# Two conditioned attention layers: where the mask of the second layer's scores is added

## The chip, the cores and the metric

The kernel runs on one core of a Trainium2 chip. The metric is the device time of one execution in microseconds. The core has five engines that work side by side and signal each other with semaphores: TensorE (matrix products; its results go to eight PSUM banks of 128 x 512 floats), VectorE, ScalarE, GpSimd, and SyncE, which issues the DMAs here. SBUF is the on-chip memory of 128 partitions.

## The reference

The input x is 64 sequences of 128 positions with 512 features. Two layers run one after the other, each x + h(x). The first is a linear attention of 8 heads. The second, which this case is about, is an ordinary softmax attention of 16 heads of 32 features:

```python
xn = layer_norm(x, norm_w, norm_b)
q = (xn @ q_w + q_b).reshape(Bx, Tx, H, -1)
k = (xn @ k_w + k_b).reshape(Bx, Tx, H, -1)
att = jnp.einsum('bnhl,bmhl->bnmh', q, k)
att = att + (1.0 - mask) * -1000000.0          # one value for each key position m
att = jax.nn.softmax(att, axis=2)              # over m
v = ((xn @ v_w + v_b) * src_mask[:, :, None]).reshape(Bx, Tx, H, -1)
y = jnp.einsum('bnmh,bmhl->bnhl', att, v).reshape(Bx, Tx, Dx)
h = layer_norm(y, sb_norm_w, sb_norm_b) * (1.0 + scale) + shift   # scale, shift from emb
h = jax.nn.silu(h) @ out_w + out_b
return x + h
```

## The kernel before

`setup` loads the small inputs, `layer0` runs the first layer and writes its result to a DRAM tensor, `second_weights` prepares the second layer's weights, and `layer1` runs the second layer. All work goes by pairs of sequences, 32 of them. Each engine has its own program, a hand-written order of steps (`body(i, ...)`), once for every pair; the steps of one pair's end (pair i - 1) are woven into the body of pair i. An engine runs its own instructions strictly in the order written.

All large products are of floats split into a high and a low part, three products instead of one (`project_features` L462 to L464, `project_rows` L453 to L455).

The scores of a sequence come twice in `layer1`. The first time (`scores`, L1475) they are laid out with the query position in the partitions: four banks (`S_BANKS`), the four row strips `a` of the array at the same time, each bank holding four heads side by side (128 columns each). Ahead of the products of the heads (`heads`, L1422), each bank is opened by a product of two rows of ones with two rows that hold the mask's high and low part (L1485, tile `mask_rows`), so that the mask is in the sum. VectorE then takes the negated maximum of every head (`maxima`, L1168, instruction at L1171) into `top`. TensorE transposes `top` (`shift_row`, L1490, product at L1493), ScalarE copies it to `top_T`, and the second time (`weight_scores`) the scores are computed transposed, opened by a product that adds the negated maxima (L1443); ScalarE's exponential adds the mask there as a per-partition bias (`mask_add`). That second part is not touched.

VectorE's body (L1238) is, in order: the row statistics of the next pair (L1136, which wait for the DMA of its rows), its normalisation, `keys_out`, then for the pair before `end_outputs` of the first sequence (it begins with the reciprocal L1178, which waits for TensorE's transposed outputs), `end_norm`, `end_outputs` of the second. Then `values` (v, L1198), and from here the steps alternate: maximum (bank 0), `end_silu` (hs, L1209), `end_norm` (z, L1204), maximum (bank 1), `low_part` (h_lo, L1213), v, maxima (banks 2, 3), `end_silu`, `x_low` (xT_lo, L1151), `low_part`, `end_add` (y_out, L1222), and for the second sequence maxima (2, 3), `x_low`, maxima (0, 1), `end_add`.

TensorE's body (L1499) starts by waiting for both xT_lo of its pair. It computes the keys, with `shift_row` of the pair before's second sequence after 16 of the products, and behind them `weight_scores`; then the queries, the outputs (`mixed`, `turned`), the values, the transposition of z (`z_transposed`, L1393, which waits for z), `scores` of the first sequence, the values of the second, the second `z_transposed`, `x_transposed` for the next pair, `out_rows` (which waits for h_lo), `x_transposed`, `scores` of the second sequence (which waits until the first four banks have been read, L1475 on), `out_rows` of the second sequence with `shift_row` in its midst.

SyncE loads the mask rows of the next pair with four small DMAs (`load_masks`, L1041), after the stores and the load of the rows of pair i + 2. That load waits until the stores of the pair before are finished.

Of the kernel before, what the change touches and what calls it, by code (L numbers as in the profile page):

```python
# [12 lines left out]
P = 128  # L13
PAIR = 2
# [21 lines left out]
def build(nc, T, out):  # L36
# [9 lines left out]
    assert S == P and D1 == 32 and D0 == 64 and NP > 4  # L46

    x1_d = nc.dram_tensor("x_between_layers", [B, S, D], F32).ap()
    mask_d = nc.dram_tensor("mask_parts", [2, 2, B, S], F32).ap()

    root = ExitStack()
    with root:
        def sem(name):
            return root.enter_context(nc.semaphore(name))

        def sb(ctx, name, shape, dt=F32):
            return ctx.enter_context(nc.sbuf_tensor(name, shape, dt))

        ps = [root.enter_context(nc.psum_tensor(f"bank{i}", [P, 512], F32)) for i in range(8)]


# [12 lines left out]
        x_in = [sem("l0_x_in"), sem("l1_x_in")]  # L74
        eps = sb(root, "eps", [P, 2])
        neg_half = sb(root, "neg_half", [P, 2])


        vec_rows = {}
        at = 0  # L80
        for name in ("L0_cond_ln_w", "L0_cond_ln_b", "L0_cond_ln2_w", "L0_cond_ln2_b", "L0_cond_b_emb",
                     "L1_cond_norm_w", "L1_cond_norm_b", "L1_cond_sb_norm_w", "L1_cond_sb_norm_b",
                     "L1_cond_emb_b", "L1_cond_q_b", "L1_cond_k_b"):
            n = T[name].shape[0] // P
            vec_rows[name] = (at, n)
            at += n
        n_vec = at

        def vcol(name, c):
            r = vec_rows[name][0] + c  # L90
            return vec[:, r:r + 1]

        mats = [[("L0_cond_Wq", "L0_cond_bq"), ("L0_cond_Wk", "L0_cond_bk"), ("L0_cond_Wv", "L0_cond_bv"),
                 ("L0_cond_W_out", "L0_cond_b_out")],
                [("L1_cond_q_w", "L1_cond_q_b"), ("L1_cond_k_w", "L1_cond_k_b"), ("L1_cond_v_w", "L1_cond_v_b"),
                 ("L1_cond_out_w", "L1_cond_out_b")]]
        raw1_in = [sem(f"raw1_in{n}") for n in range(4)]
        bias1_ps, stored0 = sem("bias1_ps"), sem("l0_stored")

        with ExitStack() as both:  # L100
            raw1 = [sb(both, f"raw1_{n}", [P, C, D]) for n in range(4)]
            with ExitStack() as ctx:
                key_bias = sb(ctx, "key_bias", [P, D], F32R)
                setup(nc, mats[0], T, sem, sb, ps, ident, ones, w_hi, w_lo, bias_all, key_bias, half_gain,
                      half_shift, vec, vec_rows, n_vec, vcol, mask_col, mask_off, mask_d, eps, neg_half, x_d, xr,
                      x_in[0], raw1, B, D, C, KE)
                layer0(nc, ctx, sem, sb, ps, x_d, x1_d, xr, x_in[0], w_hi, w_lo, ident, bias_all, key_bias,
                       half_gain, half_shift, mask_col, mask_d, eps, neg_half,
                       [T[w] for w, _ in mats[1]], raw1, raw1_in, bias1_ps,
                       [vcol("L1_cond_norm_b", c) for c in range(C)], stored0, B, NP, D, C, H0, D0)  # L110
            second_weights(nc, mats[1], T, sem, sb, ps, w_hi, w_lo, raw1, raw1_in, ones, bias_all, qk_bias, vec,
                           vec_rows, vcol, x1_d, xr, x_in[1], bias1_ps, stored0, B, D, C)

        with ExitStack() as ctx:
            layer1(nc, ctx, sem, sb, ps, x1_d, out, xr, x_in[1], w_hi, w_lo, ident, bias_all, qk_bias,
                   half_gain, half_shift, mask_col, mask_off, mask_d, eps, neg_half, B, NP, D, C, HC, H1, D1)


def high_part(nc, w_hi, raw, n, C, gain):
# [16 lines left out]


def setup(nc, mats, T, sem, sb, ps, ident, ones, w_hi, w_lo, bias_all, key_bias, half_gain, half_shift,
          vec, vec_rows, n_vec, vcol, mask_col, mask_off, mask_d, eps, neg_half, x_d, xr, x_in, emb_room, B, D, C,
          KE):  # L140


    with ExitStack() as ctx:
# [53 lines left out]
        def _(sp):  # L197
# [18 lines left out]
                load_rows(sp, x_d, xr, pair, pair, x_in)  # L216
            sp.wait_ge(mask_step, 6)
            for n, part in enumerate((mask_hi, mask_lo)):
                sp.dma_start(mask_d[:, n].rearrange("l b t -> b l t"), f32(part[:])).then_inc(mask_out, 16)
            sp.wait_ge(mask_out, 32)  # L220

        @block.gpsimd
        def _(pool):
# [271 lines left out]
def layer0(nc, ctx, sem, sb, ps, x_d, x1_d, xr, x_in, w_hi, w_lo, ident, bias_all, key_bias,  # L495
# [53 lines left out]
    def _(sp):  # L549
        sp.wait_ge(s["rows_preset"], 1)  # L550

        def load_masks(pair, slot):
            for n, r in enumerate((64, 96)):
                sp.dma_start(f32(mask_rows[r:r + 1, slot, :]),
                             mask_d[0, n, bass.ds(pair * PAIR, PAIR)].rearrange("b t -> (b t)").unsqueeze(0))\
                    .then_inc(s["masks_in"], 16)

        load_masks(0, 0)
# [418 lines left out]


def layer1(nc, ctx, sem, sb, ps, x1_d, out, xr, x_in, w_hi, w_lo, ident, bias_all, qk_bias,
           half_gain, half_shift, mask_col, mask_off, mask_d, eps, neg_half, B, NP, D, C, HC, H, DH):  # L980

    Q, K, V, O = range(4)
    BV, BO = 1, 2
# [4 lines left out]
    xT_lo = sb(ctx, "xT_lo1", [P, C, PAIR, P], F32R)  # L988

    qk = sb(ctx, "qk", [P, 2, C, PAIR, P])  # L990
    mask_rows = sb(ctx, "mask_rows1", [P, PAIR * P], F32R)
    mask_add = sb(ctx, "mask_add", [P, PAIR])
    one_rows = sb(ctx, "one_rows", [P, P], F32R)
    chunk_of = sb(ctx, "chunk_of", [P, DH])
# [25 lines left out]

    s = {n: sem("l1_" + n) for n in (
        "preset", "rows_preset", "stats", "var", "var_eps", "rstd", "xn", "xT_ps", "xT_hi", "xT_lo", "masks", "v_bias", "x_biased",
        "qk_ps", "k", "q", "masks_in", "mask_add", "v_ps", "v", "s_ps", "top", "top_ps", "top_T", "w_ps", "prob", "yT_ps", "yT", "y_ps", "p_sum", "y", "y_stats", "y_var", "y_var_eps", "y_rstd", "z",
        "z_ps", "gains", "g", "tanh", "silu", "h_hi", "h_lo", "o_ps", "out", "stored")}

    QK_BANKS = ((0, 1), (2, 3))
# [12 lines left out]
    @block.sync  # L1039
    def _(sp):  # L1040
        def load_masks(pair):  # L1041
            for a in range(HC):
                sp.dma_start(f32(mask_rows[DH * a:DH * a + 2, :]),
                             mask_d[1, :, bass.ds(pair * PAIR, PAIR)].rearrange("r b t -> r (b t)"))\
                    .then_inc(s["masks_in"], 16)

        def store(prev, b):
            sp.wait_ge(s["out"], seq(PAIR, prev + 1, b + 1))
# [4 lines left out]
        def body(i, first, more, last):  # L1053
# [5 lines left out]
                sp.wait_ge(x_in, seq(16, i, 32))  # L1059
                load_rows(sp, x1_d, xr, i + 2, (i + 2) % RING, x_in)  # L1060
            if not last:
                sp.wait_ge(s["s_ps"], seq(PAIR * C, i, PAIR * C))
                sp.wait_ge(s["masks_in"], seq(16 * HC, i, 16 * HC))
                load_masks(i + 1)

        bodies(sp, NP, body)
# [65 lines left out]
    def _(dve):  # L1132
# [33 lines left out]
                    done.then_inc(s["k"], 1)  # L1166

        def maxima(i, b, banks):  # L1168
            for a in banks:
                dve.wait_ge(s["s_ps"], seq(PAIR * C, i, b * C + S_ORDER[b].index(a) + 1))  # L1170
                nc.vector.tensor_reduce(top[:, b, DH * a:DH * a + C],  # L1171
                                        ps[S_BANKS[a]][:, :].rearrange("p (c t) -> p c t", c=C), AX_X, ALU.max,
                                        negate=True).then_inc(s["top"], 1)

        def end_outputs(prev, b):
# [206 lines left out]
    def _(pe):  # L1382
# [36 lines left out]
                yield  # L1419
            done.then_inc(s["v_ps"], 1)  # L1420

        def heads(dst, weights, moving, b, order, signal):  # L1422

            for c in range(C):
                for a in order:
                    rows = slice(DH * a, DH * a + DH)
                    last = nc.tensor.matmul(ps[dst[a]][:, c * P:(c + 1) * P], qk[rows, weights, c, b, :],  # L1427
                                            qk[rows, moving, c, b, :], start=False, stop=(c == C - 1),
                                            tile_position=(DH * a, 0))
                    if c == C - 1:  # L1430
                        last.then_inc(signal, 1)
# [1 line left out]
        def weight_scores(prev, b):  # L1433
# [7 lines left out]
            for a in range(HC):  # L1441
# [1 line left out]
                nc.tensor.matmul(ps[W_BANKS[a]][:, :], one_rows[rows, :],  # L1443
                                 top_T[rows, b].rearrange("p c t -> p (c t)"), start=True, stop=False,
                                 tile_position=(DH * a, 0))
            heads(W_BANKS, K, Q, b, range(HC), s["w_ps"])

        def mixed(prev, b):

# [25 lines left out]
        def scores(i, b, first):  # L1475

            if b == 0:
                pe.wait_ge(s["masks_in"], seq(16 * HC, i, 16 * HC))
                pe.wait_ge(s["q"], seq(2, i, 2))
                pe.wait_ge(s["k"], seq(2, i, 2))  # L1480
            else:
                pe.wait_ge(s["top"], seq(PAIR * C, i, C))
            for a in S_ORDER[b]:
                rows = slice(DH * a, DH * a + 2)
                nc.tensor.matmul(ps[S_BANKS[a]][:, :], one_rows[rows, :],  # L1485
                                 mask_rows[rows, b * P:(b + 1) * P].unsqueeze(1).broadcast_to([2, C, P]),
                                 start=True, stop=False, tile_position=(DH * a, 0))
            heads(S_BANKS, Q, K, b, S_ORDER[b], s["s_ps"])

        def shift_row(i, b):  # L1490

# [7 lines left out]
        def body(i, first, more, last):  # L1499
            pe.wait_ge(s["xT_lo"], seq(PAIR, i, PAIR))  # L1500
            for f in range(C):
                if not first and f % 2 == 0:

                    pe.wait_ge(s["top"], seq(PAIR * C, i - 1, C + f // 2 + 1))
                keys = projected(i, 1, (f,))
                if not first and f == 1:
                    run(islice(keys, 4))
# [77 lines left out]
```

## Time and profile before

| | before |
|---|---|
| median of 3 runs | 2241.32 us (2240.42 to 2241.78) |
| profiled execution | 2241.82 us, span 2240.0 us |
| TensorE products busy | 2180.2 us, 97% |
| VectorE busy | 1400.3 us, 63% |
| ScalarE busy | 906.7 us, 40% |
| GpSimd busy | 549.0 us, 25% |
| mean granted TensorE clock | 0.982 |
| second layer | from about 1054 us on |

PE is TensorE's products, PEld its weight loads, DVE VectorE, ACT ScalarE. In the timeline, a row's first number is the start in microseconds from the span's start, the second the duration; x2 at its end means two instructions merged into one row. The bracket gives the idle time of the engine before it and what ended that. PEclk is the granted clock, 1.00 for 2.4 GHz.

### The profile page before, as it was taken

The page shows a single profiled execution, that of the slowest core. Times are in us where ns is not written, and L with a number is a line of the kernel's source. Part 1 is how long each engine was busy: PE and PEld are TensorE (multiplying, and loading weights), DVE is VectorE, ACT ScalarE, POOL GpSimd, SP SyncE. Part 2 cuts the span into 40 slices and gives each one's busy share as a digit, 9 for nine tenths or more (in the row PEclk, how much of TensorE's full clock was granted, in tenths as well). Part 3 has the DMA queues.
Part 4 walks back from the last instruction along what each step waited for, and adds up shares of the span by engine and source line. Part 5 has one row for each costly group of instructions (what it writes and reads, how often), then busy time and mean ns, then how long its engine had stood idle before and what let it go on. Part 6 is the DMA issues. An engine that isn't in the chain of part 4 may idle for free.

```text
span 2240.0 us, 53652 instructions
## 1 busy us (share of the span) xinstructions
PE 2180.2 (97%) x20991; PEld 1883.2 (84%) x20991; DVE 1400.3 (63%) x3001; ACT 906.7 (40%) x2086; POOL 549.0 (25%) x879
## 2 busy tenths in 40 slices
PE   6899999999999999997999999999999999999996
PEld 3788888888888888885888888888888888888885
DVE  4677777777777777765456465555556465555544
ACT  2233333333333333333344444445444444444443
POOL 0323333332233333322121221212121221212120
PEclk9899999999999999996999999999999999999998
DMA  7211110010111100101010000101010000101000
GB/s 253 85 38 38 38 38 28 33 38 33 38 38 38 38 28 33 38 24 48 1 38 24 33 28 28 38 19 38 19 38 24 33 29 28 38 19 38 19 30 20
DMA packets 51447, 85.17 MB, mean 38 GB/s; under 512 B 5588, under 2 KB 14482, under 8 KB 51416
## 3 DMA queue, kind: packets, MB, share of 16 engines
q1 hardware_dynamic: 51416, 84.73, 10.8%
q8 instruction: 22, 0.36, 0.1%
q14 instruction: 9, 0.07, 0.0%
HBM read 51.03 MB, written 33.69 MB: 38 GB/s over the span
## 4 chain that ended last, share of the span: by engine, by line
PE 51%; DVE 1%; ACT 0%; issue 0%; DMA 0%; POOL 0%; POOLq 0%; DVEq 0%; SPq 0%
PE bank L462 6%; PE bank L453 6%; PE bank L463 6%; PE bank L464 5%; PE bank L455 5%; PE bank L454 5%; PE bank L1427 5%; PE bank L1453 3%; PE bank L1459 3%; PE bank L1470 2%; PE bank L1443 1%; PE bank L1393 1%; PE bank L1386 1%; PE bank L1485 1%; PE bank L1493 0%; ACT prob L1305 0%
## 5 line engine op out<-in xcount | busy, mean ns | idle before, releaser
L462 PE MATMUL bank<-xT_hi,w_hi 128*128 128x256 f32 x1536 | 447.0, 291 | 4.5 <-DVE xT_lo L1151 3.3
L463 PE MATMUL bank<-xT_lo,w_hi 128*128 128x256 f32 x1536 | 442.1, 288 | 0.0
L464 PE MATMUL bank<-xT_hi,w_lo 128*128 128x256 f32 x1536 | 438.9, 286 | 0.0
L453 PE MATMUL bank<-w_hi,xT_hi 128*128 128x512 f32 x768 | 318.4, 415 | 0.0
L455 PE MATMUL bank<-w_lo,xT_hi 128*128 128x512 f32 x768 | 309.7, 403 | 0.0
L462 PEld LDWEIGHTS bank<-xT_hi,w_hi 128*128 128x128 f32 x1536 | 290.7, 189 | 20.3 <-issue 8.0
L454 PE MATMUL bank<-w_hi,xT_lo 128*128 128x512 f32 x768 | 306.6, 399 | 0.0
L463 PEld LDWEIGHTS bank<-xT_lo,w_hi 128*128 128x128 f32 x1536 | 291.2, 190 | 1.2
L464 PEld LDWEIGHTS bank<-xT_hi,w_lo 128*128 128x128 f32 x1536 | 291.5, 190 | 0.0
L810 ACT ACTIVATE k_exp<-bank,k_neg 128x128 f32<-128x128 f32 x256 | 72.9, 370 | 370.6 <-DVE k_neg L695 368.6
L453 PE MATMUL bank<-w_hi,h_hi 128*128 128x512 f32 x512 | 217.4, 425 | 3.6 <-DVE h_lo L1213 3.6
L454 PE MATMUL bank<-w_hi,h_lo 128*128 128x512 f32 x512 | 206.9, 404 | 0.0
L455 PE MATMUL bank<-w_lo,h_hi 128*128 128x512 f32 x512 | 203.5, 397 | 0.0
L1305 ACT ACTIVATE prob<-bank,mask_add 128x512 f32<-128x512 f32 x256 | 154.9, 688 | 100.1 <-PE bank L1427 100.1
L453 PEld LDWEIGHTS bank<-w_hi,xT_hi 128*128 128x128 f32 x768 | 144.4, 188 | 40.7 <-issue 6.1
L455 PEld LDWEIGHTS bank<-w_lo,xT_hi 128*128 128x128 f32 x768 | 144.6, 188 | 37.0
L1096 POOL TENSOR_TENSOR xr<-xr,bias_all 128x512 f32 (+1 forms) x64 | 81.2, 1293 | 361.4 <-DVE top L1171 360.3
L454 PEld LDWEIGHTS bank<-w_hi,xT_lo 128*128 128x128 f32 x768 | 145.2, 189 | 28.9
L1171 DVE TENSOR_REDUCE top<-bank 128x4 f32<-128x512 f32 x256 | 166.6, 683 | 4.1 <-PE bank L1427 1.4
L1136 DVE BATCH_NORM_STATS2 stats<-xr 128x6 f32 (+1 forms) x64 | 41.2, 685 | 186.8 <-DMA xr<-x_between_layers 186.5
L1322 ACT ACTIVATE g<-bank,gains 128x128 f32<-128x128 f32 x256 | 96.1, 456 | 142.3 <-PE bank L1393 142.3
L606 POOL TENSOR_TENSOR h_lo<-hs,h_hi 128x512 fp32r<-128x512 f32 x64 | 86.9, 1379 | 236.9 <-ACT h_hi L836 236.9
(181 smaller groups left out, 4073.3 us busy)
## 6 DMA issues: line engine op xcount, KB each, us to landing
xr<-in_x SPq DMA_DIRECT2D x32, 512.0 KB, 3.5
x_between_layers<-x SPq DMA_DIRECT2D x64, 256.0 KB, 2.0
xr<-x_between_layers SPq DMA_DIRECT2D x32, 512.0 KB, 3.6
out<-y_out SPq DMA_DIRECT2D x64, 256.0 KB, 2.0
raw<-in_L_cond_W_emb SPq DMA_DIRECT2D x4, 1024.0 KB, 12.2
raw<-in_L_cond_emb_w SPq DMA_DIRECT2D x4, 1024.0 KB, 8.3
mask_rows<-mask_parts SPq DMA_DIRECT2D x128, 2.0 KB
raw<-in_L_cond_Wq SPq DMA_DIRECT2D x1, 1024.0 KB, 5.4
```

The lines of the kernel that those rows point to most:

```text
L453: yield nc.tensor.matmul(bank[:, :], a_hi[:, c, b, :], w_hi[:, m, c, :], start=(c == 0), stop=False)
L454: yield nc.tensor.matmul(bank[:, :], a_lo[:, c, b, :], w_hi[:, m, c, :], start=False, stop=False)
L455: yield nc.tensor.matmul(bank[:, :], a_hi[:, c, b, :], w_lo[:, m, c, :], start=False, stop=(c == C - 1))
L462: yield nc.tensor.matmul(dst, w_hi[:, m, c, fs], a_hi[:, c], start=(first and c == 0), stop=False)
L463: yield nc.tensor.matmul(dst, w_hi[:, m, c, fs], a_lo[:, c], start=False, stop=False)
L464: yield nc.tensor.matmul(dst, w_lo[:, m, c, fs], a_hi[:, c], start=False, stop=(c == C - 1))
L606: nc.gpsimd.tensor_tensor(h_lo[:, :, b, :], hs[:, b], f32(h_hi[:, :, b, :]), ALU.subtract).then_inc(s["h_lo"], 1)
L1096: last = nc.gpsimd.tensor_tensor(xr[:, slot, b], xr[:, slot, b], bias_all[:, BO, :], ALU.add)
L1171: nc.vector.tensor_reduce(top[:, b, DH * a:DH * a + C], ps[S_BANKS[a]][:, :].rearrange("p (c t) -> p c t", c=C), AX_X, ALU.max, negate=Tru ...
L1305: nc.scalar.activation(prob[:, b].rearrange("p (c a) t -> p c a t", c=C)[:, :, a, :], ps[W_BANKS[a]][:, :].rearrange("p (c t) -> p c t", c=C),
L1322: last = nc.scalar.activation(g[:, b, c, :], ps[Z_BANKS[b]][:, c * P:(c + 1) * P], ACT.Identity, scale=gains[:, 0, c, b:b + 1], bias=gains ...
L1427: last = nc.tensor.matmul(ps[dst[a]][:, c * P:(c + 1) * P], qk[rows, weights, c, b, :], qk[rows, moving, c, b, :], start=False, stop=(c == ...
```

## The change

The mask of the second layer goes from TensorE to VectorE. In the setup, the mask of the second layer is written to DRAM once, as plain floats (`mask_f`), next to the split parts that the first layer still uses. In `layer1`, one DMA a pair brings the two rows of a pair into all 128 partitions (`mask_wide`). `scores` has no row products any more; the products of the heads start their parts of the bank themselves. `maxima` adds the bank and the mask into one of two SBUF tiles (`masked`) and takes the maximum from there. The waits for a bank to be free (L1475 on, and the keys of the next pair) now are for that add and no longer for the maximum. The next mask load waits for the last maximum of the pair.

```diff
@@ setup, sync
             for n, part in enumerate((mask_hi, mask_lo)):
-                sp.dma_start(mask_d[:, n].rearrange("l b t -> b l t"), f32(part[:])).then_inc(mask_out, 16)
-            sp.wait_ge(mask_out, 32)
+                sp.dma_start(mask_d[n], f32(part[:, 0, :])).then_inc(mask_out, 16)
+            sp.dma_start(mask_f, mask_in[:, 1, :]).then_inc(mask_out, 16)
+            sp.wait_ge(mask_out, 48)
@@ layer1
-    mask_rows = sb(ctx, "mask_rows1", [P, PAIR * P], F32R)
+    mask_wide = sb(ctx, "mask_wide", [P, PAIR, P])
+    masked = sb(ctx, "masked", [P, 2, C, P])
@@ layer1, sync
         def load_masks(pair):
-            for a in range(HC):
-                sp.dma_start(f32(mask_rows[DH * a:DH * a + 2, :]),
-                             mask_d[1, :, bass.ds(pair * PAIR, PAIR)].rearrange("r b t -> r (b t)"))\
-                    .then_inc(s["masks_in"], 16)
+            sp.dma_start(mask_wide[:], mask_f[bass.ds(pair * PAIR, PAIR)].unsqueeze(0).broadcast_to([P, PAIR, P]))\
+                .then_inc(s["masks_in"], 16)
...
             if not last:
-                sp.wait_ge(s["s_ps"], seq(PAIR * C, i, PAIR * C))
-                sp.wait_ge(s["masks_in"], seq(16 * HC, i, 16 * HC))
+                sp.wait_ge(s["masks_in"], seq(16, i, 16))
+                sp.wait_ge(s["top"], seq(PAIR * C, i, PAIR * C))
                 load_masks(i + 1)
@@ layer1, vector
         def maxima(i, b, banks):
+            if b == 0 and 0 in banks:
+                dve.wait_ge(s["masks_in"], seq(16, i, 16))
             for a in banks:
-                dve.wait_ge(s["s_ps"], seq(PAIR * C, i, b * C + S_ORDER[b].index(a) + 1))
-                nc.vector.tensor_reduce(top[:, b, DH * a:DH * a + C],
-                                        ps[S_BANKS[a]][:, :].rearrange("p (c t) -> p c t", c=C), AX_X, ALU.max,
+                done = b * C + S_ORDER[b].index(a) + 1
+                dve.wait_ge(s["s_ps"], seq(PAIR * C, i, done))
+                nc.vector.tensor_tensor(masked[:, a % 2], ps[S_BANKS[a]][:, :].rearrange("p (c t) -> p c t", c=C),
+                                        mask_wide[:, b].unsqueeze(1).broadcast_to([P, C, P]),
+                                        ALU.add).then_inc(s["masked"], 1)
+                dve.wait_ge(s["masked"], seq(PAIR * C, i, done))
+                nc.vector.tensor_reduce(top[:, b, DH * a:DH * a + C], masked[:, a % 2], AX_X, ALU.max,
                                         negate=True).then_inc(s["top"], 1)
@@ layer1, tensor
-        def heads(dst, weights, moving, b, order, signal):
+        def heads(dst, weights, moving, b, order, signal, opened):
...
-                                            qk[rows, moving, c, b, :], start=False, stop=(c == C - 1),
+                                            qk[rows, moving, c, b, :], start=not opened,
+                                            stop=not opened or c == C - 1,
...
         def scores(i, b, first):
             if b == 0:
-                pe.wait_ge(s["masks_in"], seq(16 * HC, i, 16 * HC))
                 pe.wait_ge(s["q"], seq(2, i, 2))
                 pe.wait_ge(s["k"], seq(2, i, 2))
             else:
-                pe.wait_ge(s["top"], seq(PAIR * C, i, C))
-            for a in S_ORDER[b]:
-                rows = slice(DH * a, DH * a + 2)
-                nc.tensor.matmul(ps[S_BANKS[a]][:, :], one_rows[rows, :],
-                                 mask_rows[rows, b * P:(b + 1) * P].unsqueeze(1).broadcast_to([2, C, P]),
-                                 start=True, stop=False, tile_position=(DH * a, 0))
-            heads(S_BANKS, Q, K, b, S_ORDER[b], s["s_ps"])
+                pe.wait_ge(s["masked"], seq(PAIR * C, i, C))
+            heads(S_BANKS, Q, K, b, S_ORDER[b], s["s_ps"], False)
@@ layer1, tensor, body (keys)
                 if not first and f % 2 == 0:
-                    pe.wait_ge(s["top"], seq(PAIR * C, i - 1, C + f // 2 + 1))
+                    pe.wait_ge(s["masked"], seq(PAIR * C, i - 1, C + f // 2 + 1))
```

## Rows read from the trace of the kernel before

**Rows 1.** View by windows (columns: window, length, busy of each engine, PEclk, DMA, GB/s).

```profile
1080.00:1090.00 10.00, 7.19 (x76) 6.01 (x74) 7.17 (x15) 2.73 (x8) 1.43 (x2) 1.00 0.00 1
1400.00:1800.00 400.00, 400.00 (x4907) 351.14 (x4907) 228.19 (x459) 188.66 (x424) 82.60 (x156) 1.00 0.08 29
```

**Rows 2.** VectorE's timeline (start us, us, engine, line, operation, tiles, [idle before <-releaser]).

```profile
1613.29 0.26 DVE L1178 RECIPROCAL p_sum<-bank 128x16 f32<-128x16 f32 x1 [2.10 <-PE bank L1470]
...
1634.52 1.29 DVE L1136 BATCH_NORM_STATS2 stats<-xr 128x6 f32 x2 [6.46 <-DMA xr<-x_between_layers]
...
1643.70 0.26 DVE L1178 RECIPROCAL p_sum<-bank 128x16 f32<-128x16 f32 x1 [3.88 <-PE bank L1470]
...
1649.27 0.26 DVE L1178 RECIPROCAL p_sum<-bank 128x16 f32<-128x16 f32 x1 [2.11 <-PE bank L1470]
...
1651.22 0.75 DVE L1198 SCALAR_TENSOR_TENSOR v<-bank,mask_now,v_bias 128x512 f32<-128x512 f32 x1
1651.88 0.68 DVE L1171 TENSOR_REDUCE top<-bank 128x4 f32<-128x512 f32 x1
1652.60 0.69 DVE L1209 SCALAR_TENSOR_TENSOR hs<-th,g 128x512 f32<-128x512 f32 x1
1653.21 0.54 DVE L1204 TENSOR_SCALAR z<-z,mv_y,rstd_y 128x512 f32<-128x512 f32 x1
...
1654.27 0.69 DVE L1213 TENSOR_TENSOR h_lo<-hs,h_hi 128x512 fp32r<-128x512 f32 x1
...
1655.53 1.28 DVE L1171 TENSOR_REDUCE top<-bank 128x4 f32<-128x512 f32 x2
1657.37 0.69 DVE L1209 SCALAR_TENSOR_TENSOR hs<-th,g 128x512 f32<-128x512 f32 x1 [0.56 <-ACT th L1328]
...
1658.76 0.69 DVE L1213 TENSOR_TENSOR h_lo<-hs,h_hi 128x512 fp32r<-128x512 f32 x1
1659.37 0.68 DVE L1222 TENSOR_TENSOR y_out<-bank,xr 128x512 f32<-128x512 f32 x1
1660.14 1.29 DVE L1171 TENSOR_REDUCE top<-bank 128x4 f32<-128x512 f32 x2
1661.35 0.68 DVE L1151 TENSOR_TENSOR xT_lo<-bank,xT_hi 128x512 fp32r<-128x512 f32 x1
1661.95 1.28 DVE L1171 TENSOR_REDUCE top<-bank 128x4 f32<-128x512 f32 x2
1663.36 0.69 DVE L1222 TENSOR_TENSOR y_out<-bank,xr 128x512 f32<-128x512 f32 x1
```

**Rows 3.** Timeline, weight loads of TensorE (PEld) behind a wait, same body.

```profile
1654.30 0.59 PEld L1393 LDWEIGHTS bank<-ident,z 128*128 128x128 f32 x4
...
1655.30 0.19 PEld L453 LDWEIGHTS bank<-w_hi,h_hi 128*128 128x128 f32 x1
...
1660.05 0.19 PEld L453 LDWEIGHTS bank<-w_hi,h_hi 128*128 128x128 f32 x1
...
1662.82 0.19 PEld L462 LDWEIGHTS bank<-xT_hi,w_hi 128*128 128x128 f32 x1
...
1664.86 0.14 PEld L1493 LDWEIGHTS bank<-ident,top 128*128 128x128 f32 x1
```

**Rows 4.** Line L1485, the mask's row products, and TensorE's timeline at the second scores.

```profile
L1485 PE MATMUL bank<-mask_rows,one_rows x256: 491/494/498, 1077.3 to 2197.8; 2*128 2x512 f32 x128
...
1658.72 0.51 PE L1485 MATMUL bank<-mask_rows,one_rows 2*128 2x512 f32 x4
...
1659.06 1.06 PE L1427 MATMUL bank<-qk 32*128 32x128 f32 x32
```

**Rows 5.** VectorE's timeline in the first layer: an add and a maximum of it.

```profile
607.75 0.69 DVE L703 TENSOR_TENSOR q_exp<-bank,bias_all 128x512 f32<-128x512 f32 x1 [0.57 <-PE bank L455]
608.47 0.69 DVE L705 TENSOR_REDUCE q_max<-q_exp 128x8 f32<-128x512 f32 x1
```

**Rows 6.** Timeline of ScalarE, the second h_hi of the same body.

```profile
1658.10 0.63 ACT L1332 ACTIVATE h_hi<-hs 128x512 fp32r<-128x512 f32 x1 [0.27 <-DVE hs L1209]
```

More of the change, by code:

```diff
@@ L48, in build @@
     x1_d = nc.dram_tensor("x_between_layers", [B, S, D], F32).ap()
-    mask_d = nc.dram_tensor("mask_parts", [2, 2, B, S], F32).ap()
+    mask_d = nc.dram_tensor("mask_parts", [2, B, S], F32).ap()
+    mask_f = nc.dram_tensor("mask_second", [B, S], F32).ap()
     root = ExitStack()
@@ L104, in build @@
                 setup(nc, mats[0], T, sem, sb, ps, ident, ones, w_hi, w_lo, bias_all, key_bias, half_gain,
-                      half_shift, vec, vec_rows, n_vec, vcol, mask_col, mask_off, mask_d, eps, neg_half, x_d, xr,
+                      half_shift, vec, vec_rows, n_vec, vcol, mask_col, mask_off, mask_d, mask_f, eps, neg_half, x_d, xr,
                       x_in[0], raw1, B, D, C, KE)
@@ L115, in build @@
             layer1(nc, ctx, sem, sb, ps, x1_d, out, xr, x_in[1], w_hi, w_lo, ident, bias_all, qk_bias,
-                   half_gain, half_shift, mask_col, mask_off, mask_d, eps, neg_half, B, NP, D, C, HC, H1, D1)
+                   half_gain, half_shift, mask_col, mask_off, mask_f, eps, neg_half, B, NP, D, C, HC, H1, D1)
 def high_part(nc, w_hi, raw, n, C, gain):
@@ L138, in setup @@
 def setup(nc, mats, T, sem, sb, ps, ident, ones, w_hi, w_lo, bias_all, key_bias, half_gain, half_shift,
-          vec, vec_rows, n_vec, vcol, mask_col, mask_off, mask_d, eps, neg_half, x_d, xr, x_in, emb_room, B, D, C,
+          vec, vec_rows, n_vec, vcol, mask_col, mask_off, mask_d, mask_f, eps, neg_half, x_d, xr, x_in, emb_room, B, D, C,
           KE):
@@ L554, in load_masks @@
                 sp.dma_start(f32(mask_rows[r:r + 1, slot, :]),
-                             mask_d[0, n, bass.ds(pair * PAIR, PAIR)].rearrange("b t -> (b t)").unsqueeze(0))\
+                             mask_d[n, bass.ds(pair * PAIR, PAIR)].rearrange("b t -> (b t)").unsqueeze(0))\
                     .then_inc(s["masks_in"], 16)
@@ L979, in layer1 @@
 def layer1(nc, ctx, sem, sb, ps, x1_d, out, xr, x_in, w_hi, w_lo, ident, bias_all, qk_bias,
-           half_gain, half_shift, mask_col, mask_off, mask_d, eps, neg_half, B, NP, D, C, HC, H, DH):
+           half_gain, half_shift, mask_col, mask_off, mask_f, eps, neg_half, B, NP, D, C, HC, H, DH):
     Q, K, V, O = range(4)
@@ L1022, in layer1 @@
         "preset", "rows_preset", "stats", "var", "var_eps", "rstd", "xn", "xT_ps", "xT_hi", "xT_lo", "masks", "v_bias", "x_biased",
-        "qk_ps", "k", "q", "masks_in", "mask_add", "v_ps", "v", "s_ps", "top", "top_ps", "top_T", "w_ps", "prob", "yT_ps", "yT", "y_ps", "p_sum", "y", "y_stats", "y_var", "y_var_eps", "y_rstd", "z",
+        "qk_ps", "k", "q", "masks_in", "mask_add", "v_ps", "v", "s_ps", "masked", "top", "top_ps", "top_T", "w_ps", "prob", "yT_ps", "yT", "y_ps", "p_sum", "y", "y_stats", "y_var", "y_var_eps", "y_rstd", "z",
         "z_ps", "gains", "g", "tanh", "silu", "h_hi", "h_lo", "o_ps", "out", "stored")}
@@ L1445, in weight_scores @@
                                  tile_position=(DH * a, 0))
-            heads(W_BANKS, K, Q, b, range(HC), s["w_ps"])
+            heads(W_BANKS, K, Q, b, range(HC), s["w_ps"], True)
         def mixed(prev, b):
```

## Prediction

> **What bounds the kernel now.** I read the view by windows first. In 1400 to 1800 us, the middle of the second layer, TensorE is busy all 400 us and VectorE 228 us [rows 1]. That says TensorE is the bound and that VectorE has 172 us to spare. An average cannot say where in a body that spare time lies, so the second view is VectorE's timeline over one body (one pair of batch elements), and the third is the weight loads at which TensorE would have to wait for VectorE.
>
> A body takes 1649.27 - 1613.29 = 35.98 us [rows 2]. VectorE's spare time is mostly in two places: before the row statistics, where it waits 6.46 us for the next rows, and before the first reciprocal (3.88 us) [rows 2]. From the reciprocal at 1649.27 to the last maximum, which ends at 1661.95 + 1.28 = 1663.23, it is nearly without a pause; the only idle time shown is 0.56 us before the second hs [rows 2]. All eight maxima of a body, where the change adds its work, lie inside this dense stretch. So the question is not whether VectorE has room in a body but how late each of its results may come before TensorE waits for it.
>
> Those margins, each from the end of the VectorE result to the weight load of TensorE that needs it [rows 2, 3]: h_lo of the first element ends 1654.27 + 0.69 = 1654.96 and is used at 1655.30 (0.34 us). The second h_lo ends 1659.45, used 1660.05 (0.60). The second xT_lo ends 1662.03, used when the next body starts at 1662.82 (0.79). The last maximum ends 1663.23, used by the transposition of `top` at 1664.86 (1.63).
>
> **What the change takes off TensorE.** Two groups of four row products a body, 256 products in 32 bodies, so 64 groups [rows 4]. The four run side by side in four row strips. From the first of a group to the first score product is 1659.06 - 1658.72 = 0.34 us [rows 4]. If nothing else moved, TensorE would save 64 x 0.34 = 21.8 us. The score products now start their banks themselves; their number and shapes stay, so I cost that at nothing. If switching from full-array work to strips needs part of the 0.34 us anyway, the saving is smaller (nothing at the lower end).
>
> **What it adds on VectorE.** One add of 128x512 before each maximum (scores in a bank plus a tile in SBUF, result in SBUF), and a wait for that add ahead of the maximum. The first layer has just this sequence: an add that reads a bank and an SBUF tile (0.69 us), then a maximum over its SBUF result 608.47 - 607.75 = 0.72 us later, itself 0.69 us long [rows 5]. So the maximum from SBUF costs what the maximum from a bank costs now (0.68) [rows 2], and each add moves what is behind it by 0.72 us: 8 x 0.72 = 5.76 us a body. Bounds: 0.68, if the gap vanished, and 0.78, if the add cost the 0.75 us of the v instruction plus the gap of 0.03 [rows 2]. The second input repeats one row of 128 for the four heads; I cost that at nothing, with the 0.78 as its cover.
>
> The Trainium skill (VectorE: DVE Perf Modes, section on the TRN2 errata) gives a VectorE instruction 120 fixed cycles from PSUM and 58 from SBUF. By that the maxima would each be 62 / 0.96 = 65 ns shorter than now, an estimate. By it the sum would be lower by 8 x 0.065 = 0.52 us a body, some 2329 us in all. The rows of the first layer speak against it.
>
> **Following one body.** I keep the clock of the trace and let the body begin with the second reciprocal at 1649.27, which waits for TensorE.
>
> - The v instruction at 1651.22 is unmoved. Add and maximum one: +0.72, of which 0.11 was waiting already (the step from the maximum at 1651.88 to hs at 1652.60 is 0.72 where 0.61 is the step without a wait). After the second, h_lo is late by 1.33, so it ends at 1656.29.
> - TensorE, 0.34 us ahead by then, first waits for the second z (normalised at 1653.21, now late by 0.61, so ready at 1654.36, where TensorE comes to it at 1654.30 - 0.34 = 1653.96), 0.44 us, and then for h_lo until 1656.33 instead of passing at 1655.30. It is 1.03 us late.
> - Adds three and four bring VectorE to +2.77 at the fourth maximum. The idle time before the second hs absorbs 0.63 (the step there is 1.24 from the second of the two maxima begun at 1655.53), leaving 2.14. The second h_lo starts at 1658.76 when ScalarE's h_hi, from 1658.10 for 0.63 us, is done [rows 6], and h_hi follows hs, so nothing is absorbed there: it ends at 1661.58 instead of 1659.45. TensorE, which saved another 0.34 us at the second scores, would have passed at 1660.76 and passes at 1661.62, 1.57 late.
> - The step from y_out at 1659.37 to the maxima at 1660.14 has 0.17 of waiting. Adds five and six give 2.14 - 0.17 + 1.44 = 3.41; the second xT_lo ends at 1665.43, and the next body starts at 1665.5 instead of 1662.82, 2.7 late.
> - Adds seven and eight: 4.85. The last maximum ends at 1668.08 and the transposition of `top` starts at 1668.12 instead of 1664.86: **3.26 us late**.
>
> From there to the next second reciprocal, 1685.25, TensorE's work is as before and waits for nothing new: the body grows from 35.98 to about 39.24 us. The short form: 5.76 added, 0.91 absorbed by waits in the dense stretch, 1.59 by the margin at the last maximum (1.63 less 0.04 for the signal). The 0.68 us saved on TensorE lie wholly inside the waiting. TensorE will stand about 3.26 + 0.68 = 3.94 us a body.
>
> **Other queues.** y_out ends VectorE's body at 1663.36 + 0.69 = 1664.05. It now waits 0.2 us for its bank (1.41 behind the two maxima at 1661.95, where two steps of 0.60 are 1.20), so it ends 4.63 later. Behind it are the store, the next load of rows and the row statistics; relative to TensorE these are 4.63 - 3.26 = 1.37 us later, which the idle 3.88 us before the first reciprocal cover [rows 2]. Without that cover they would cost up to 1.37 us a body. SyncE's four mask loads a body become one, spread over the partitions, issued after all maxima of the body; it is issued right behind the load of the rows, which has landed when the row statistics start at 1634.52, and the first add needs it where the first maximum is now, at 1651.88 [rows 2]. So it costs nothing; its cover is those 17 us. On SyncE only the next body's stores stand behind it, which wait for later results. The extra store of the mask in the setup is one DMA; at most a microsecond once.
>
> **The sum.** 32 bodies x 3.26 = 104.3 us; the first and last bodies, which lack some of this work, I count as the others. On the profiled execution's 2241.8 us (span 2240.0 and 1.8 around it; 0.5 above the median of the runs) that gives **2346 us**. By the bounds of the add: 0.68 gives 2.94 a body and 2336; 0.78 gives 3.74 and 2362.
>
> **Rivals.**
> 1. *The saving stays and VectorE's spare time hides the adds* (faster; the other side of my forecast). 2241.8 - 21.8 = 2220 us. For it: 172 us of 400 spare. Against it: the spare time is ahead of the dense stretch, and the narrowest margin is 0.34 us against 1.33 us of delay. It decides at a delay of 1.6 + 0.9 = 2.5 us over the eight adds, 0.31 us each; no VectorE instruction over 512 elements in the rows is near that. Chance 0.04.
> 2. *Part of the delay is hidden by a mechanism I do not see* (a maximum that starts before its add has fully ended, the SBUF maximum shorter): 2 us a body or less, 2245 to 2306 us. Chance 0.07, of which 0.02 within 0.2%.
> 3. *The waits bring TensorE's clock down.* It stands 10% of the time, in five pieces of up to 1.1 us. In 1080 to 1090 us it stood nearly 3 of 10 us and the granted clock stayed at 1.00, the 2.4 GHz level [rows 1]. Should a quarter of TensorE's 20.4 us a body from the transposition of `top` on run at 1.2 GHz, that adds up to 5.1 us a body, 2346 + 163 = 2509. Chance 0.05.
> 4. *More waits than I traced* (the weight-score products of the next body wait for y_out, which ends 4.63 later while TensorE is only 3.26 late; a restart of TensorE may cost a few tenths): one us a body more, 2378. Chance 0.10.
>
> The change does what it says in the diff (the row products are gone, the add is there), so no chance goes to that.
>
> **How the numbers follow.** My case has 0.74 and by its bounds 2336 to 2362. The range takes in the page's value and a part of rival 4: 2318 to 2372, which holds about 8 in 10. A measurement of this kernel can tell 0.2%, 4.5 us, from no change; faster by more 0.04, within 0.02, slower by more 0.94.
>
> **What would show it.** In the changed kernel's profile: body period near 39.2 us; add and maximum 0.72 us apart, both about 0.69; VectorE busy some 177 us more (256 x 0.69); TensorE waiting on VectorE at five places a body, on z, twice on h_lo, on xT_lo and on top; no row products of the mask. A maximum from SBUF much under 0.68, or a period near 35.3 with TensorE unbroken, would prove me wrong; a granted clock under 1.00 in 1400 to 1800 us would point to rival 3.

## The result and the profile after

The changed kernel takes 2343.74 us (median of 4 runs, 2342.06 to 2344.51) against 2241.55 us before (4 runs): ratio 1.0456, 95% interval 1.0444 to 1.0469. The forecast was 2346 us, in a range of 2318 to 2372. The profiled execution has a span of 2342.7 us at a mean granted clock of 0.981 (before 2240.0 at 0.982).

The view by windows, 1400 to 1800 us (window, length, busy of TensorE's products, weight loads, VectorE, ScalarE, GpSimd, PEclk, DMA share, GB/s), of the changed kernel, beside [rows 1]:

```profile
1400.00:1800.00 400.00, 372.84 (x4436) 317.19 (x4435) 260.71 (x500) 171.08 (x389) 77.28 (x144) 1.00 0.09 31
```

TensorE is no longer busy throughout (372.84 of 400 us) and neither is VectorE. No engine is full; what has grown is waiting. The granted clock is 1.00 as before, so the clock has no part in it in this stretch.

VectorE's timeline of one body, as [rows 2], from the second reciprocal to the second reciprocal of the next body:

```profile
1699.92 0.26 DVE L1185 RECIPROCAL p_sum<-bank 128x16 f32<-128x16 f32 x1 [2.11 <-PE bank L1478]
...
1701.87 0.75 DVE L1205 SCALAR_TENSOR_TENSOR v<-bank,mask_now,v_bias 128x512 f32<-128x512 f32 x1
1702.53 0.68 DVE L1175 TENSOR_TENSOR masked<-bank,mask_wide 128x512 f32<-128x512 f32 x1
1703.25 0.69 DVE L1179 TENSOR_REDUCE top<-masked 128x4 f32<-128x512 f32 x1
1703.85 0.68 DVE L1216 SCALAR_TENSOR_TENSOR hs<-th,g 128x512 f32<-128x512 f32 x1
...
1710.12 0.68 DVE L1216 SCALAR_TENSOR_TENSOR hs<-th,g 128x512 f32<-128x512 f32 x1
1710.72 0.68 DVE L1152 TENSOR_TENSOR xT_lo<-bank,xT_hi 128x512 fp32r<-128x512 f32 x1
1711.50 0.69 DVE L1220 TENSOR_TENSOR h_lo<-hs,h_hi 128x512 fp32r<-128x512 f32 x1
1712.11 0.69 DVE L1229 TENSOR_TENSOR y_out<-bank,xr 128x512 f32<-128x512 f32 x1
1712.71 0.68 DVE L1175 TENSOR_TENSOR masked<-bank,mask_wide 128x512 f32<-128x512 f32 x1
...
1717.98 0.69 DVE L1179 TENSOR_REDUCE top<-masked 128x4 f32<-128x512 f32 x1
1718.58 0.68 DVE L1229 TENSOR_TENSOR y_out<-bank,xr 128x512 f32<-128x512 f32 x1
...
1733.49 0.26 DVE L1185 RECIPROCAL p_sum<-bank 128x16 f32<-128x16 f32 x1 [2.76 <-PE bank L1478]
...
1739.06 0.26 DVE L1185 RECIPROCAL p_sum<-bank 128x16 f32<-128x16 f32 x1 [2.11 <-PE bank L1478]
```

The body is 1739.06 - 1699.92 = 39.14 us, 3.16 more than the 35.98 of before. Between the add at 1702.53 and its maximum lie 0.72 us. No row from the v instruction to y_out has a bracket of idle time any more: the dense stretch, v to the end of the last maximum, is 1718.67 - 1701.87 = 16.80 us, where it was 12.01. The idle time that is left stands where it did nobody any good before either, ahead of the reciprocals.

The weight loads of TensorE that were preceded by idle time, same body, as [rows 3]:

```profile
1705.11 0.42 PEld L1400 LDWEIGHTS bank<-ident,z 128*128 128x128 f32 x4 [0.42 <-issue]
...
1706.96 0.19 PEld L455 LDWEIGHTS bank<-w_hi,h_hi 128*128 128x128 f32 x1 [1.00 <-DVE h_lo L1220]
...
1712.24 0.19 PEld L455 LDWEIGHTS bank<-w_hi,h_hi 128*128 128x128 f32 x1 [0.87 <-DVE h_lo L1220]
...
1716.17 0.19 PEld L464 LDWEIGHTS bank<-xT_hi,w_hi 128*128 128x128 f32 x1 [1.20 <-issue]
...
1718.72 0.14 PEld L1495 LDWEIGHTS bank<-ident,top 128*128 128x128 f32 x1 [0.58 <-DVE top L1179]
```

Five places, one after the other: the second z, h_lo twice, xT_lo and top. (Two brackets say "issue" as releaser; z of VectorE ends 0.12 us and xT_lo 0.14 us before these loads.)

### The profile page after: what moved, and what is told of

Same layout as the page of the kernel before. It is cut to its first block, busy times and chain, and to the rows that moved or that the text cites. A ratio compares the mean times of both kernels' runs of the same rounds, so it can differ in the third digit from the quotient of the medians.

```text
span 2342.7 us, 53217 instructions
## 1 busy us (share of the span) xinstructions
PE 2198.1 (94%) x20735; PEld 1868.8 (80%) x20735; DVE 1563.6 (67%) x3257; ACT 903.3 (39%) x2086; POOL 548.5 (23%) x879
## 4 chain that ended last, share of the span: by engine, by line
PE 29%; DVE 18%; issue 7%; ACT 1%; DVEq 0%; DMA 0%; POOL 0%; POOLq 0%; SPq 0%
DVE masked L1175 7%; PE bank L464 5%; PE bank L465 5%; PE bank L466 4%; PE bank L1461 3%; PE bank L1434 3%; PE bank L1467 2%; DVE top L1179 2%; DVE hs L1216 2%; PE bank L1478 1%; PE bank L455 1%; PE bank L1451 1%; PE bank L456 1%; PE bank L457 1%; DVE v L1205 1%
## 5 line engine op out<-in xcount | busy, mean ns | idle before, releaser
L464 PE MATMUL bank<-xT_hi,w_hi 128*128 128x256 f32 x1536 | 450.6, 293 | 28.5 <-DVE xT_lo L1152 27.3
L464 PEld LDWEIGHTS bank<-xT_hi,w_hi 128*128 128x128 f32 x1536 | 291.2, 190 | 55.9 <-issue 44.8
L1179 DVE TENSOR_REDUCE top<-masked 128x4 f32<-128x512 f32 x256 | 175.6, 686 | 8.9
L1175 DVE TENSOR_TENSOR masked<-bank,mask_wide 128x512 f32<-128x512 f32 x256 | 174.0, 680 | 0.3 <-PE bank L1434 0.3
L455 PEld LDWEIGHTS bank<-w_hi,h_hi 128*128 128x128 f32 x512 | 97.3, 190 | 82.5 <-DVE h_lo L1220 63.0
```

The source lines that it names most:

```text
L455: yield nc.tensor.matmul(bank[:, :], a_hi[:, c, b, :], w_hi[:, m, c, :], start=(c == 0), stop=False)
L464: yield nc.tensor.matmul(dst, w_hi[:, m, c, fs], a_hi[:, c], start=(first and c == 0), stop=False)
L1175: nc.vector.tensor_tensor(masked[:, a % 2], ps[S_BANKS[a]][:, :].rearrange("p (c t) -> p c t", c=C), mask_wide[:, b].unsqueeze(1).broadcas ...
L1179: nc.vector.tensor_reduce(top[:, b, DH * a:DH * a + C], masked[:, a % 2], AX_X, ALU.max, negate=True).then_inc(s["top"], 1)
```

## The experiments

Each was compared with the kernel before, run on the same chip. Where a body's period is given, it is the distance of two second reciprocals in VectorE's timeline. The diffs show the part that matters: where a maximum reads its bank directly, TensorE's wait for that bank to be free is for the maximum instead of the add, and experiment 2 also brings back the loads of the mask rows. The maxima lack the mask where there is no add (experiments 1 and 9, half of them in 3 and 4) and in 7 and 8.

### 1. The change without its adds

```diff
@@ maxima, against the changed kernel
-                nc.vector.tensor_tensor(masked[:, a % 2], ps[S_BANKS[a]][:, :].rearrange("p (c t) -> p c t", c=C),
-                                        mask_wide[:, b].unsqueeze(1).broadcast_to([P, C, P]),
-                                        ALU.add).then_inc(s["masked"], 1)
-                dve.wait_ge(s["masked"], seq(PAIR * C, i, done))
-                nc.vector.tensor_reduce(top[:, b, DH * a:DH * a + C], masked[:, a % 2], AX_X, ALU.max,
+                nc.vector.tensor_reduce(top[:, b, DH * a:DH * a + C],
+                                        ps[S_BANKS[a]][:, :].rearrange("p (c t) -> p c t", c=C), AX_X, ALU.max,
                                         negate=True).then_inc(s["top"], 1)
```

> The changed kernel without the eight adds a body: the row products of the mask are gone from TensorE, and the maxima are taken straight from the banks, without the mask (the exponential still adds it). What the change would give if VectorE's part cost nothing. By the 0.34 us a group of the prediction 64 x 0.34 = 21.8 us less than before, 2220 us. By the changed kernel's trace (from the weight loads of the z transposition to those of the values 1.86 us, before 2.08) a group was worth only 0.22: 64 x 0.22 = 14 us, 2227 us. Rival: switching to the strips costs as much as the products did, 2241 us.

Measured: 2225.96 us, ratio 0.9936 (0.9920 to 0.9953). TensorE is busy again without a gap:

```profile
1400.00:1800.00 400.00, 400.00 (x4909) 351.67 (x4908) 228.44 (x460) 190.07 (x429) 86.24 (x159) 1.00 0.10 34
```

So the saving on TensorE is real, 14.4 us, but two thirds of the 21.8 that I had reckoned. Why, the weight loads around the first scores show. Before:

```profile
1649.54 0.59 PEld L1393 LDWEIGHTS bank<-ident,z 128*128 128x128 f32 x4
1650.29 0.19 PEld L1485 LDWEIGHTS bank<-mask_rows,one_rows 2*128 2x128 f32 x4 [0.17 <-issue]
1650.40 1.10 PEld L1427 LDWEIGHTS bank<-qk 32*128 32x128 f32 x32
1651.62 0.19 PEld L453 LDWEIGHTS bank<-w_hi,xT_hi 128*128 128x128 f32 x1
```

and in the changed kernel:

```profile
1700.18 0.59 PEld L1400 LDWEIGHTS bank<-ident,z 128*128 128x128 f32 x4
1700.94 0.98 PEld L1434 LDWEIGHTS bank<-qk 32*128 32x128 f32 x32 [0.17 <-issue]
1702.04 0.19 PEld L455 LDWEIGHTS bank<-w_hi,xT_hi 128*128 128x128 f32 x1
```

From the transposition of z to the values it was 2.08 us and is now 1.86, so a group was worth 0.22 us: 64 x 0.22 = 14.1. The timeline of TensorE's products in the changed kernel shows where the other 0.12 of my 0.34 went:

```profile
1700.94 1.17 PE L1434 MATMUL bank<-qk 32*128 32x128 f32 x32
```

From the first of the heads' products to the next block it is 1702.04 - 1700.94 = 1.10 us now. Behind the row products it was 1660.05 - 1659.06 = 0.99 [rows 3, 4]. Whatever comes first in the strips pays some 0.11 us here, and that was in the step I read.

### 2. The products put back, the adds kept

```diff
@@ scores, against the changed kernel
+            for a in S_ORDER[b]:
+                rows = slice(DH * a, DH * a + 2)
+                nc.tensor.matmul(ps[S_BANKS[a]][:, :], one_rows[rows, :],
+                                 mask_rows[rows, b * P:(b + 1) * P].unsqueeze(1).broadcast_to([2, C, P]),
+                                 start=True, stop=False, tile_position=(DH * a, 0))
-            heads(S_BANKS, Q, K, b, S_ORDER[b], s["s_ps"], False)
+            heads(S_BANKS, Q, K, b, S_ORDER[b], s["s_ps"], True)
```

> The changed kernel with the row products of the mask put back on TensorE, adds kept (the mask is added twice). My theory: TensorE's work is inside its waiting for VectorE, so putting back 64 groups costs nothing: 2344 us as the changed kernel, within 2 us. Rival: TensorE's work counts as well, 2344 + 14 = 2358, or + 22 = 2366 us.

Measured: 2344.06 us, ratio 1.0459 (1.0442 to 1.0476), the changed kernel's time. The view by waits, 1400 to 1800 us (who <- for whom: us in total, times, longest), of the changed kernel

```profile
PEld bank L455 <- DVE h_lo L1220: 18.8, 20, 1.0
```

and of this one

```profile
PEld bank L457 <- DVE h_lo L1228: 16.4, 20, 1.0
```

The same for the transposition of z, the changed kernel first:

```profile
PEld bank L1400 <- issue: 4.2, 10, 0.4
```

```profile
PEld bank L1408 <- issue: 2.0, 10, 0.2
```

The work put back is taken out of the waiting: 2.4 and 2.2 us over some ten bodies are 0.46 us a body, two groups of 0.22. Once VectorE sets the pace, what is spared on TensorE is worth nothing; the whole of the 118 us between experiment 1 and the changed kernel belongs to the adds.

### 3 and 4. Adds for one sequence of the pair only

```diff
@@ maxima, against the changed kernel (experiment 3; in 4 it is b == 1)
+                if b == 0:
+                    nc.vector.tensor_tensor(masked[:, a % 2], ps[S_BANKS[a]][:, :].rearrange("p (c t) -> p c t", c=C),
+                                            mask_wide[:, b].unsqueeze(1).broadcast_to([P, C, P]),
+                                            ALU.add).then_inc(s["masked"], 1)
...
+                    src = masked[:, a % 2]
+                else:
+                    src = ps[S_BANKS[a]][:, :].rearrange("p (c t) -> p c t", c=C)
```

> Adds only for the first sequence of a pair (four a body), the maxima of the second straight from the banks, without the mask; no row products. My theory: the waits at the two h_lo set the time, VectorE's last maximum comes soon enough: TensorE passes the second h_lo 1.57 us late and keeps that, 31 x 1.57 + some 2 at the ends, 2292 us. Rival: only VectorE's total counts, each add the same, half of 102 us: 2293 us. The two agree here and part in the next run. Rival: what binds is the last maximum alone, 4 adds x 0.72 - 0.91 - 1.59 = 0.38 a body, 2254 us.

> Adds only for the second sequence of a pair (four a body), the maxima of the first straight from the banks, without the mask; no row products. My theory: nothing before the second xT_lo is late; that one ends 1.3 to 1.4 us later against 0.79 of margin, the last maximum 2.8 us later against 1.63: TensorE is 1.2 us late a body, 31 x 1.2 = 37, 2279 us. Rival, only VectorE's total counts: 2293 us. Rival: the h_lo waits do all the harm, then this run is near 2230.

Measured: 2289.33 us, ratio 1.0217 (1.0200 to 1.0234), with the adds in the first sequence, and 2273.25 us, ratio 1.0146 (1.0129 to 1.0163), with them in the second. The same work of VectorE costs 63 us over experiment 1 in the one place and 47 in the other, so its total alone doesn't decide. Waits of TensorE in 1400 to 1800 us with the adds first:

```profile
PEld bank L455 <- DVE h_lo L1224: 20.8, 22, 1.0
PE bank L455 <- DVE h_lo L1224: 16.1, 22, 0.8
```

and with the adds second:

```profile
PEld bank L464 <- issue: 12.0, 21, 0.9
PEld bank L1499 <- DVE top L1183: 6.4, 11, 0.6
PE bank L464 <- DVE xT_lo L1152: 5.2, 11, 0.5
```

The first has the waits for h_lo (and 4.7 us ahead of the transposition of z, 0.4 a body, as the changed kernel has), the second only those for xT_lo and top, as expected. The body with the adds first is 37.53 us long (1708.66 to 1746.19), 1.55 over before, for which 1.57 was worked out. With the adds second it is 36.85, 0.87 over before, not the 1.2 of the expectation. I had left VectorE's steps at their old times there, but the second hs follows ScalarE's tanh, and that follows the transposition of z, which now comes 0.22 us sooner; 1.2 less 0.22 is nearly what was measured. The trace bears this out. The second hs of this kernel:

```profile
1708.03 0.69 DVE L1220 SCALAR_TENSOR_TENSOR hs<-th,g 128x512 f32<-128x512 f32 x1 [0.35 <-ACT th L1339]
```

It starts 7.90 us behind the second reciprocal at 1700.13; before it was 8.10, with 0.56 us of idle time ahead of it [rows 2]. The second xT_lo ends 1.06 us later than before and the last maximum 2.50, where 1.3 to 1.4 and 2.8 were expected.

### 5. The last maximum is asked for later

```diff
@@ TensorE's body, keys, against the changed kernel
-                if not first and f == 1:
-                    run(islice(keys, 4))
-                    shift_row(i - 1, 1)
                 run(keys)
+                if not first and f == 1:
+                    shift_row(i - 1, 1)
```

> The changed kernel, with the transposition of the second sequence's maxima eight products later in TensorE's keys (at the end of the second quarter, right before the weight-score products). That is 0.95 us more margin for the last maximum; all else as it was. My theory: the last maximum no longer sets the body, the second xT_lo does, 2.66 us late instead of 3.2: 31 x 0.5 = 17 us less than the changed kernel, 2327 us. Rival: the dense stretch of VectorE is the bound whatever TensorE's order, 2344 us. Rival: all of the 0.95 is gained, 2315 us.

Measured: 2327.87 us, ratio 1.0384 (1.0367 to 1.0402); 15.9 us less than the changed kernel's 2343.7. The body is 38.56 us (2.58 over before). There is no wait for top any more, and the one for xT_lo is as long as it was:

```profile
PEld bank L464 <- issue: 14.1, 21, 1.2
PE bank L464 <- DVE xT_lo L1152: 8.4, 11, 0.8
...
PEld bank L1451 <- DVE y_out L1229: 1.8, 11, 0.2
```

Of 0.95 us of new margin 0.58 is gained, just what the wait for top was; then xT_lo binds. VectorE's program is the same in both kernels, so its dense stretch is not a bound by itself: where TensorE asks for its last result decides. A new wait is there too, for y_out, at the weight-score products.

### 6. And xT_lo made earlier

```diff
@@ VectorE's body, against experiment 5
-            maxima(i, 1, (2, 3))
             if not last:
                 x_low(i + 1, 1)
+            maxima(i, 1, (2, 3))
```

> As the run before, and VectorE makes the second xT_lo ahead of the maxima of the second sequence instead of between them. My theory: xT_lo is then ready before TensorE comes, the wait at the start of the body goes, and the last maximum binds again, with its larger margin: 3.2 - 0.95 = 2.3 us a body over before, 2241.5 + 71 = 2313 us. Rival: as the run before, 2327 us (then it was not xT_lo).

Measured: 2325.98 us, ratio 1.0374 (1.0355 to 1.0391). The 14 us that I expected did not come. The wait for xT_lo has gone as it should, but TensorE now waits behind it:

```profile
1708.98 0.14 PEld L1495 LDWEIGHTS bank<-ident,top 128*128 128x128 f32 x1 [0.66 <-DVE top L1179]
1709.57 0.19 PEld L1451 LDWEIGHTS bank<-top_T,one_rows 4*128 4x128 f32 x4 [0.46 <-DVE y_out L1229]
```

```profile
1708.84 0.68 DVE L1229 TENSOR_TENSOR y_out<-bank,xr 128x512 f32<-128x512 f32 x1
```

y_out ends at 1709.52, and the weight-score products start at 1709.57. They write the bank that y_out is read from. I had looked only at the last maximum as the end of the dense stretch, but the last result that TensorE needs of it is y_out. All of the stretch lies before that wait, so its inner order no longer helps.

### 7 and 8. Smaller adds

```diff
@@ maxima, against the changed kernel (n = 1 in experiment 7, 2 in 8; four heads to a bank)
+                bank = ps[S_BANKS[a]][:, :].rearrange("p (c t) -> p c t", c=C)
+                nc.vector.tensor_tensor(masked[:, a % 2, 0:n, :], bank[:, 0:n, :],
+                                        mask_wide[:, b].unsqueeze(1).broadcast_to([P, n, P]),
                                         ALU.add).then_inc(s["masked"], 1)
                 dve.wait_ge(s["masked"], seq(PAIR * C, i, done))
-                nc.vector.tensor_reduce(top[:, b, DH * a:DH * a + C], masked[:, a % 2], AX_X, ALU.max,
+                nc.vector.tensor_reduce(top[:, b, DH * a:DH * a + C], bank, AX_X, ALU.max,
                                         negate=True).then_inc(s["top"], 1)
```

> As the changed kernel, but each add covers one head of four (128 columns) and its result is not used: the maximum still waits for it and then reads the bank, without the mask; TensorE waits for the maximum. An add of 128 columns takes 0.28 us (the first layer's z instruction) plus 0.03 for the signal: 0.31 us each, the point at which the prediction put the decision. My theory, with 0.22 us a group saved on TensorE: the first h_lo makes TensorE 0.17 us late, later margins keep it at about 0.2 us a body, 2241.7 + 6 = 2248 us. Rival, proportional to VectorE's added time (8 x 0.31 of 8 x 0.72): 2226 + 118 x 0.43 = 2277 us. Rival: small adds hide wholly, 2226 us.

> As the run before with adds of 256 columns (two heads of four). 0.68 - 256 / 0.96 ns = 0.41 us, plus 0.03: 0.44 us each. My theory: the second xT_lo and the last maximum each make TensorE 1.0 us late a body, 2241.7 + 31 x 1.05 + 1 = 2275 us. Rival, proportional: 2226 + 118 x 0.61 = 2298 us.

Measured: 2251.14 us, ratio 1.0038 (1.0024 to 1.0052), and 2278.67 us, ratio 1.0162 (1.0147 to 1.0178). The adds took 281 and 415 ns (VectorE's groups in 1400 to 1800 us):

```profile
L1176 DVE TENSOR_TENSOR masked<-bank,mask_wide 128x128 f32<-128x128 f32 x88 | 24.7, 281 | 0.0
```

```profile
L1176 DVE TENSOR_TENSOR masked<-bank,mask_wide 128x256 f32<-128x256 f32 x88 | 36.5, 415 | 0.0
```

The bodies are 36.20 and 37.05 us: 0.22 and 1.07 over before, where 0.2 and 1.05 were worked out. Over the 30 steps from body to body that is 6.6 and 32 us; what is left of the difference to before, 2 and 4 us, lies outside them.

Which margin holds TensorE up in experiment 7, the trace shows, in one body (second reciprocal at 1691.26):

```profile
1697.52 0.19 PEld L455 LDWEIGHTS bank<-w_hi,h_hi 128*128 128x128 f32 x1 [0.42 <-DVE h_lo L1221]
...
1702.04 0.50 PE L455 MATMUL bank<-w_hi,h_hi 128*128 128x512 f32 x1
...
1705.15 0.19 PEld L464 LDWEIGHTS bank<-xT_hi,w_hi 128*128 128x128 f32 x1 [0.40 <-issue]
```

TensorE waits for the first h_lo and is late there, but the second group saved brings it level again: the product at 1702.04 comes 10.78 us behind the reciprocal, just as before (1660.05 - 1649.27). Then it waits for the second xT_lo, which ends 0.14 us ahead of the load at 1705.15, and from there it is 0.2 us late. There is no wait for top. So xT_lo makes this body longer.

The four points, by what an add moves its followers:

| per add | time | over experiment 1 |
|---|---|---|
| 0 | 2226.0 us | 0 |
| 0.31 us | 2251.1 us | 25 us |
| 0.44 us | 2278.7 us | 53 us |
| 0.72 us | 2343.7 us | 118 us |

Shared out over 31 bodies, it is 65 us for 0.28 us from 0.44 to 0.72: 65 / 31 / 0.28 = 7.5 us of time for each microsecond of an add, near the eight adds of a body in full. Up to 0.31 it is 25 / 31 / 0.31 = 2.6. The margins swallow the first part. The point at which the kernel is as fast as before lies under 0.31 us; no run stands on it. By an estimate from xT_lo's margin it is 0.28 us: six adds, less the 0.91 us of waits that absorb some of it, against 0.79 less 0.04 us for the signal, (0.75 + 0.91) / 6.

### 9. The mask left to the exponential

Without the row products, the adds, and the loads of the mask for them:

```diff
@@ against experiment 1
-            sp.dma_start(mask_f, mask_in[:, 1, :]).then_inc(mask_out, 16)
...
-            sp.dma_start(mask_wide[:], mask_f[bass.ds(pair * PAIR, PAIR)].unsqueeze(0).broadcast_to([P, PAIR, P]))\
-                .then_inc(s["masks_in"], 16)
...
-                load_masks(i + 1)
```

> Neither row products nor adds nor the loads and the store of the mask for them: the maximum is over all keys, masked ones too, and the mask enters by the exponential's bias alone, as it does already. The softmax is the same for any shift, so nothing of the computation is lost as long as a masked key's score is not some 80 above the best unmasked one. Theory: the same as the first experiment, 2226 us, since the mask loads had no one waiting for them. Rival: the loads cost something, then up to 2 us less, 2224 us.

Measured: 2226.64 us, ratio 0.9931 (0.9917 to 0.9944): the same as experiment 1 within their spread, so the mask's way through DRAM into all partitions cost nothing. This kernel beats both. The maximum serves only to keep the exponential in range, and the mask still enters at its bias; with the condition in the expectation nothing is left out of the softmax.

## Why the prediction was right

- **What bounds.** The average (172 us to spare on VectorE) was rightly not taken as an answer; the margins at the waits were. All five waits are in the trace after, in the places named.
- **Price of an add.** 0.72 us for adding and waiting, from the first layer's pair [rows 5]; measured 0.72 and 0.71. The maximum from SBUF takes 0.69, as that row said. The Trainium skill (VectorE: DVE Perf Modes, section on the TRN2 errata) would have made it 65 ns shorter than from PSUM, 2329 us by that estimate. The trace of after does not agree: 686 ns mean from SBUF, 683 from the bank before.

```profile
L1179 DVE TENSOR_REDUCE top<-masked 128x4 f32<-128x512 f32 x256 | 175.6, 686 | 8.9
```

- **Following the body.** The waits worked out and measured, in us, at the weight loads: z 0.44 and 0.42; first h_lo 0.93 and 1.00; second h_lo 0.86 and 0.87; xT_lo 1.1 and 1.20; top 0.6 and 0.58. The dense stretch was to be 12.01 + 4.85 = 16.86 and is 16.80.
- **The sum.** 3.26 a body worked out, 3.16 measured. The 30 steps between the first and the last second reciprocal (1109.57 to 2188.97 us before, 1112.92 to 2286.86 after) grew by 94.5 us. The profiled executions differ by 102.7; of the other 8.2, 3.4 lie ahead of these steps and 4.8 behind them. I had counted the two ends as two more bodies, 6.5 us. The medians differ by 102.2, against 104.3 in the sum: the body a little too long and the ends a little too short cancel in part. A slip in the working, TensorE at 1660.76 where its terms give 1660.74, changes nothing.
- **What was off: the saving on TensorE.** The step from the first of the row products to the first score product, 0.34 us [rows 4], is not what a group costs; 0.22 is (experiment 1). The prediction had named the reason as its lower end, that the switch to strips needs part of it anyway. It made no difference to the sum, since the saving lay inside the waiting (experiment 2). Rival 1's 2220 us would have been 2227.
- **The point of decision.** 0.31 us an add was worked out from the wait for top alone, as if the last wait had to be the narrowest. It was a little too high: at that size the kernel is 0.4% slower than before, and its trace has no wait for top but one for the second xT_lo (experiment 7). By the prediction's own rows xT_lo already decides at 0.28.
- **The other rivals.** The clock did not fall in the steady bodies (1.00 in 1400 to 1800 us, with TensorE busy 93%). It fell once, in the first body, for some 3 us; that cost about 1.5 of the 3.4 us ahead of the steps (last section), so rival 3 was there, but small. The wait behind y_out named in rival 4 is not in the changed kernel, but it is the next one: experiments 5 and 6 ran into it.
- **Other queues.** The rows' DMA and its followers were to be covered by the idle time before the first reciprocal; 2.76 us of it are left of 3.88.
- **A sign that did not come.** VectorE was to be busy some 177 us more; it is 163 (1563.6 against 1400.3 us). Nothing in the sum rests on it.

## What to carry to other kernels

An engine with 40% of its time free can still be the one that sets the pace: take the margin of each of its results at the engine that waits, and follow the added time through them in order. Price an added instruction by a row of the same form elsewhere in the trace, with the step to the one that depends on it and not its duration alone. And ask first whether the step needs the operand at all: here the mask was not needed in the maximum, on any engine.

## What the runs showed of the hardware that was not expected

A group of four row products in the strips of TensorE, seen as 0.34 us between two starts, was worth only 0.22 us when it was taken away, because the first group in the strips pays something of its own. 
In the first body of the changed kernel TensorE stood still for 3.01 us until xT_lo was there, and the granted clock fell right behind that:

```profile
1089.11 0.38 PE L464 MATMUL bank<-xT_hi,w_hi 128*128 128x256 f32 x1 [3.01 <-DVE xT_lo L1152]
```

```profile
1080.00:1090.00 10.00, 5.11 (x53) 3.90 (x53) 9.51 (x16) 2.33 (x6) 0.00 (x0) 0.97 0.00 0
1090.00:1092.50 2.50, 2.50 (x14) 2.50 (x14) 2.46 (x5) 0.00 (x0) 0.65 (x1) 0.50 0.00 0
```

0.50 is the lower level, 1.2 GHz. From product to product of L464 it was 0.64 us there and 0.36 again behind 1092.98. Against the kernel before, where the same wait was 1.79 us and the clock stayed at 1.00, TensorE was 1.83 us late when it started these products and 3.34 when the clock was back, so the clock took some 1.5 us. In 1400 to 1800 us, at 93% busy, with weight loads waiting up to 1.2 us in every body, the clock stayed at 1.00.
